# The latent attention layer's opening, started in the layer before and made by halves of the tokens

## The reference, cut to what matters

```
ql = x @ Wqd
q = (ql @ Wqu).reshape(b, t, H, HD).transpose(0, 2, 1, 3)
qr = (ql @ Wqr).reshape(b, t, H, RD).transpose(0, 2, 1, 3)
qr = _apply_rope(qr, cos, sin)          # x*cos + rotate_half(x)*sin
ckv = x @ Wkvd
k = (ckv @ Wku)...; v = (ckv @ Wvu)...
kr = _apply_rope((x @ Wkr)[:, None], cos, sin)[:, 0]
scores = (q·k + qr·kr) * scale, causal; softmax; @ v; @ Wo
```

## Time and profile before

| | us |
|---|---|
| median of three runs | 1404.51 |
| lowest, highest | 1404.14, 1405.84 |
| the profiled execution's own time | 1405.04 |
| its span, first to last instruction | 1403.3 |
| TensorE busy in the span | 1334.0 (95%) |
| latent layer's block starts (trace time) | 976.83 |
| first score chunk of the lead on TensorE | 996.89 |
| first key scores, where the steady loop begins | 1014.26 |

### The profile page before, as it was taken

One profiled execution on the slowest core, in us unless ns is written; L12 is line 12 of the kernel. 1 busy time (PEld: TensorE's weight loads), 2 busy tenths in 40 slices (PEclk: granted clock), 3 DMA queues, 4 the chain that ended last, 5 costly groups with the idle time before them and its releaser, 6 DMA issues. The chain is left out here.

```text
span 1403.3 us, 33400 instructions
## 1 busy us (share of the span) xinstructions
PE 1334.0 (95%) x13987; PEld 754.0 (54%) x13995; DVE 897.1 (64%) x2171; ACT 685.8 (49%) x1035; POOL 278.0 (20%) x343
## 2 busy tenths in 40 slices
PE   8999999999679989999999999999899999999999
PEld 4455556475346775644555564446355555674436
DVE  4899994756486457759999845333656556535331
ACT  5587787646483225546777842111544444442110
POOL 5331513001330000053000000111533433200210
PEclk9999999999879999999999999999999999999999
DMA  4323300000300000032222030001200000000000
GB/s 94 69 37 67 71 8 3 34 1 2 121 1 5 17 1 16 1 63 37 37 36 37 9 113 0 1 0 31 42 14 17 15 14 16 7 2 0 0 0 30
DMA packets 33527, 37.51 MB, mean 27 GB/s; under 512 B 8722, under 2 KB 24194, under 8 KB 33378
## 3 DMA queue, kind: packets, MB, share of 16 engines
q1 hardware_dynamic: 33376, 35.38, 12.3%
q10 hardware_dynamic: 2, 0.00, 0.0%
HBM read 18.43 MB, written 1.07 MB: 14 GB/s over the span
## 5 line engine op out<-in xcount | busy, mean ns | idle before, releaser
L722 DVE TENSOR_REDUCE row_max_pieces<-psum 128x1 f32<-128x512 f32 (+3 forms) x672 | 407.0, 646 | 104.6 <-PE psum L604 102.7
L825 ACT ACTIVATE probs<-psum 128x1024 f32<-128x1024 f32 (+7 forms) x384 | 343.2, 900 | 200.1 <-PE psum L604 199.6
L663 PE MATMUL psum<-probs,v_ones 128*32 128x256 f32 (+1 forms) x2880 | 236.4, 362 | 8.7 <-POOL probs L593 4.3
L604 PE MATMUL psum<-q_all,k_head 97*32 97x512 f32 (+3 forms) x1536 | 177.1, 487 | 0.0
L604 PE MATMUL psum<-k_stack,q_stack 96*32 96x512 bf16 x2048 | 160.2, 380 | 3.4 <-issue 3.3
L604 PE MATMUL psum<-q_stack,k_stack 97*32 97x512 bf16 x2048 | 158.0, 379 | 2.0 <-issue 1.8
L663 PEld LDWEIGHTS psum<-probs,v_ones 128*32 128x32 f32 x2880 | 95.6, 109 | 87.7 <-POOL probs L593 24.2
L604 PEld LDWEIGHTS psum<-k_stack,q_stack 96*32 96x32 bf16 x2048 | 57.6, 96 | 66.6 <-DVE row_max_pieces L722 13.2
L604 PE MATMUL psum<-k_head_bf,q_all_bf 80*32 80x512 bf16 (+3 forms) x768 | 84.1, 329 | 3.2 <-ACT k_head_bf L2800 1.0
L604 PEld LDWEIGHTS psum<-q_stack,k_stack 97*32 97x32 bf16 x2048 | 58.5, 96 | 51.7 <-ACT probs L825 4.3
L604 PEld LDWEIGHTS psum<-q_all,k_head 97*32 97x32 f32 x1536 | 76.0, 109 | 18.1 <-issue 2.0
(11 more groups left out here) (398 smaller groups left out, 2085.9 us busy)
## 6 DMA issues: line engine op xcount, KB each, us to landing
q_stack<-arena SPq DMA_DIRECT2D x32, 96.0 KB, 2.7
k_stack<-arena SPq DMA_DIRECT2D x32, 96.0 KB, 3.0
arena<-gd_g_sums SPq DMA_DIRECT2D x6, 512.0 KB, 6.0
k_stack<-arena SPq DMA_DIRECT2D x32, 64.0 KB, 2.7
q_stack<-arena SPq DMA_DIRECT2D x32, 64.0 KB, 2.7
x_tokens<-in_x SPq DMA_DIRECT2D x4, 256.0 KB, 3.7
k_stack<-arena SPq DMA_DIRECT2D x32, 32.0 KB, 2.0
q_stack<-arena SPq DMA_DIRECT2D x32, 32.0 KB, 2.7
```

The source lines that it names most:

```text
L604: last = pe.matmul(o[j:j + 32], by[:, j:j + 32], rows, **flags)
L663: last = pe.matmul(psum[32 * g:32 * g + VW, PVB, first * P:end * P].rearrange("p (b n) -> p b n", n=P), V[:, c, h, :], by_group(pr[:, n % ...
L722: last = dve.reduce_max(mx[:, h % 2, qt, i:i + 1], o[:, 0:plain], AX.X)
L825: act.activation(pr[:, n % PB, q_from(c):], psum[:, 2 * (n % 2):2 * (n % 2) + 2, :].rearrange("p a n -> p (a n)")[:, q_from(c):], ACT.Exp, ...
```

## The change

Four things, all in code that is written out by hand:

1. `LatentEarly` takes the place of `latent_early`. The rotary query weights and the cosine and sine table are loaded with the latent weights at the start of the routed layer instead of at the start of the latent layer. VectorE turns the rotary weights (`rotate_weights`) in the routed layer, between the last product of the experts' loop and the low-rank down part. The tile `lora_down_second` is dropped, `mask_differences` is used in its place.
2. The latents of the first half of the tokens are made at the end of the routed layer, where `keep_busy` stood.
3. `Prep` is ordered by halves: keys' rotary part, head 0's rotary queries, plain features, casts and the copies of head 0's plain rows for the first 512 tokens, then for the other 512. The first four chunks need the first half only; `wait_rest_of_first` stands before m = 4.
4. Head 1's rotary queries are made after m = 1 in the lead, heads 2 and 3 after m = 5 and m = 9 (were 3 and 7). The values are made after m = 2, and the second plain features after m = 6 (was 5). Of the filler matmuls whose result nobody reads, the two of L2756 go, and of the six of `BUSY` three stay, 256 columns wide instead of 512. The engines' calls `pe_first`, `dve_first` and `act_first` are folded into `pe`, `dve` and `act`.

The diff, cut to its core:

```diff
+                    if m == NT // 2 and rope:
+                        head_loads.wait_rest_of_first(pe)
...
                 if prep:
-                    prep.pe(pe)
-                if rope:
-                    for h in rope.FIRST:
-                        rope_in(h)
-                        prep.pe_first(pe, h)
+                    prep.pe(pe, rope_in)
...
-            d1 = sb2("lora_down_second", [P, S])
+            d1 = MD
...
-            norm = Norm(core, tag, tmp2) if out_dram is None else None
+            norm = Norm(core, tag, tmp2, early=next_layer.early) if out_dram is None else None
...
                             dve.wait_ge(kept, 2 * TOPK * NH2)
+                    if next_layer:
+                        next_layer.rotate_weights(dve)
 
...
+class LatentEarly:
...
+    def loads(self, sp):
+        d = self.d
+        sp.dma_start(self.w1[:, :, 0:3 * LAT], d["w1"].rearrange("(k p) n -> p k n", p=P)).then_inc(self.loaded, 16)
+        for rows in (slice(0, LAT), slice(LAT, P)):
+            sp.dma_start(self.wq[rows, :, 0:RD], d["wqr"].rearrange("p (h n) -> p h n", n=RD)).then_inc(self.loaded, 16)
+        sp.dma_start(self.wplain[0:LAT], d["wqu"]).then_inc(self.loaded, 16)
+        sp.dma_start(self.wplain[LAT:], d["wku"]).then_inc(self.loaded, 16)
+        sp.dma_start(self.cs[:], d["cs"]).then_inc(self.loaded, 16)
+
+    def rotate_weights(self, dve):
+
+        dve.wait_ge(self.loaded, 96)
+        hf, w1, wq = RD // 2, self.w1, self.wq
+        kr, krr = w1[:, :, 2 * LAT:2 * LAT + RD], w1[:, :, 2 * LAT + RD:]
+        dve.tensor_scalar(krr[:, :, 0:hf], kr[:, :, hf:], -1.0, None, ALU.mult)
+        dve.tensor_copy(krr[:, :, hf:], kr[:, :, 0:hf])
+        dve.tensor_scalar(wq[:, :, RD:RD + hf], wq[:, :, hf:RD], -1.0, None, ALU.mult)
+        dve.tensor_copy(wq[:, :, RD + hf:], wq[:, :, 0:hf])
+
+    def latents(self, pe, half):
+
+        for k in range(KT):
+            last = pe.matmul(self.core.psum[:, half, :], self.w1[:, k, 0:2 * LAT],
+                             self.core.XNT[:, k, half * HALF:(half + 1) * HALF], start=(k == 0), stop=(k == KT - 1))
+        last.then_inc(self.l_in, 1)
+
+    def early(self, pe, half):
+        pe.wait_ge(self.loaded, 96)
+        self.latents(pe, half)
...
-                        last.then_inc(kr_in, 1)
+                def key_rotary(pe, half):
+                    if half:
+                        pe.wait_ge(kr_cs, half)
+                    for k in range(KT):
+                        last = pe.matmul(psum[:, KR_BANK, :], w1[:, k, 2 * LAT:], XNT[:, k, cols(half)],
+                                         start=(k == 0), stop=(k == KT - 1))
+                    last.then_inc(kr_in, 1)
+
+                @staticmethod
+                def pe(pe, rope_in):
+                    Prep.key_rotary(pe, 0)
+                    pe.wait_ge(l_out, 1)
+                    rope_in(0, (0,))
+                    for u in (1, 0):
+                        Prep.plain(pe, u, 0)
+                    early.latents(pe, 1)
+                    Prep.key_rotary(pe, 1)
                     pe.wait_ge(l_out, 2)
...
-                    for _ in range(2):
-                        pe.matmul(psum[:, 7, :], ident[:], XNT[:, 0, 0:HALF], start=True, stop=True)
+                    pe.wait_ge(l2_out, 1)
+                    rope_in(0, (1,))
+                    for u in (1, 0):
+                        Prep.plain(pe, u, 1)
+                    pe.wait_ge(kr_cs, 2)
...
                 @staticmethod
                 def pe_between(pe, m):
                     if m in BUSY:
-                        pe.matmul(psum[:, 7, :], ident[:], XNT[:, 0, 0:HALF], start=True, stop=True)
-                    if m == 5:
+                        pe.matmul(psum[:, 7, 0:D], ident[:], XNT[:, 0, 0:D], start=True, stop=True)
+                    if m == 2:
+                        Prep.values(pe)
+                    if m == 6:
                         pe.wait_ge(v_kept, 4)
...
-                def act(act):
+                def act(act, move_rope):
                     for half in range(NH2):
                         act.wait_ge(l_in, half + 1)
                         act.activation(L[:, cols(half)], psum[:, half, :], ACT.Copy).then_inc(l_out, 1)
-                    for half in range(NH2):
                         act.wait_ge(kr_cs, half + 1)
                         act.activation(moved[:, half, :], t[RD:, half, :], ACT.Copy).then_inc(kr_moved, 1)
...
+                        if half == 0:
+                            move_rope(0, (0,))
+                        for u in (1, 0):
+                            Prep.keep_half(act, u, half)
+                        act.wait_ge(kr_added, half + 1)
+                        act.activation(Kb[0:RD, 0, cols(half)], K[0:RD, 0, cols(half)], ACT.Copy).then_inc(kr_copied, 1)
+                    move_rope(0, (1,))
+                    act.activation(Kb[0:RD, 1, :], K[0:RD, 0, :], ACT.Copy).then_inc(kr_copied, 1)
+                    move_rope(1)
...
+                    def cast(half):
+                        for u in (1, 0):
+                            dve.wait_ge(f_kept, NH2 * half + 2 - u)
+                            out, out_b, f = PLAIN[u]
+                            dve.tensor_copy(out_b[:, f, cols(half)], out[:, f, cols(half)]).then_inc(f_cast, 1)
+
+                    by_cs(0)
+                    roped(0, (0,))
+                    add_moved(0)
+                    cast(0)
+                    dve.wait_ge(l_out, 2)
+                    dve.tensor_copy(L2[LAT:, cols(1)], psum[0:LAT, 1, :]).then_inc(l2_out, 1)
+                    by_cs(1)
+                    add_moved(1)
+                    roped(0, (1,))
+                    cast(1)
                     dve.wait_ge(masks_made, 2)
 
                 @staticmethod
...
                                        pattern=[[-1, P]], channel_multiplier=1).then_inc(masks_made, 1)
+                    pool.wait_ge(masks_made, 2)
+                    pool.memset(K[NOPE:SHIFT, :, :], 0.0).then_inc(pads, 1)
+                    pool.wait_ge(pads, 1)
+                    Rope.add(pool, 0, 0)
+                    pool.wait_ge(cast, 1)
+                    pool.memset(K[SHIFT:SHIFT + 1, :, :], 1.0).then_inc(pads, 1)
+                    pool.wait_ge(pads, 2)
+                    Rope.add(pool, 0, 1)
+                    pool.wait_ge(cast, 2)
                     pool.memset(V[:, :, :, HD + 1:], 0.0).then_inc(pads, 1)
-                    pool.memset(V[:, :, :, HD:HD + 1], 1.0).then_inc(pads, 1)
-                    for h in (*Rope.FIRST, *Rope.BETWEEN.values()):
+                    pool.wait_ge(pads, 3)
+                    for h in Rope.BETWEEN.values():
                         for half in range(NH2):
                             Rope.add(pool, h, half)
+                        if h == 1:
+                            pool.wait_ge(cast, NH2 * (h + 1))
+                            pool.memset(V[:, :, :, HD:HD + 1], 1.0).then_inc(pads, 1)
+                            pool.wait_ge(pads, 4)
                     for u in (2, 3):
                         out, out_b, f = PLAIN[u]
                         pool.wait_ge(f_kept, 2 * (u + 1))
                         pool.tensor_copy(out_b[:, f, :], out[:, f, :]).then_inc(f_cast, 1)
...
-            BUSY = range(0, 11, 2)
+            BUSY = (4, 8, 10)
...
-                FIRST, BETWEEN, AT, AHEAD = (0, 1), {3: 2, 7: 3}, 5, 4
...
+                FIRST, BETWEEN, AT, AHEAD = (0,), {1: 1, 5: 2, 9: 3}, 5, 4
...
+                def rows_of_first(sp, half):
+                    for n, (o, f) in enumerate(((Kb, kTb), (Qb, qTb))):
+                        sp.wait_ge(f_cast, NH2 * half + n + 1)
+                        sp.dma_start(o[NOPE:QROWS, 0, cols(half)], f[0:HD, 0, cols(half)]).then_inc(first_rows[half], 16)
...
+                    for half in range(NH2):
+                        HeadLoads.rows_of_first(sp, half)
+                    HeadLoads.keys_bf16(sp, 1)
+                    HeadLoads.queries(sp, 1)
                     sp.wait_ge(q_zeroed, 16)
+                    sp.dma_start(Q[NOPE:QROWS, 0, :], qT[0:HD, 0, :]).then_inc(first_q, 16)
                     sp.wait_ge(pads, 2)
-                    sp.wait_ge(f_cast, 1)
-                    for h in range(2):
-                        HeadLoads.keys_bf16(sp, h)
-                    sp.wait_ge(f_cast, 2)
-                    for h in range(2):
-                        HeadLoads.queries(sp, h)
                     for h in range(2):
                         HeadLoads.keys(sp, h)
                     for h in range(2, 4):
...
-                        pe.wait_ge(kr_copied, 2)
-                    pe.wait_ge(kb_in[h % 2], 16 * (h // 2 + 1))
-                    pe.wait_ge(q_plain[h % 4], 32 * (h // 4 + 1))
+                        pe.wait_ge(kr_copied, 1)
+                        pe.wait_ge(first_rows[0], 32)
+                        pe.wait_ge(cast, 1)
+                        return
+                    if h == 1:
```

(12 more changed lines are left out.)

174 lines of the change are left out of this document (57 added, 117 removed).

## The result

| | before | after |
|---|---|---|
| median on the same chip, us | 1404.10 (eight runs) | 1408.57 (eight runs) |
| lowest, highest | 1401.81, 1405.84 | 1403.47, 1413.23 |
| the profiled execution's own time, its span | 1405.04, 1403.3 | 1405.14, 1403.4 |
| mean granted clock of that execution | 0.984 | 0.979 |
| block's start to first row maximum | 20.35 | 11.2 |

The ratio of after to before is 1.0035, interval 1.0022 to 1.0048: slower by 0.35%, where 0.55% faster was forecast. The opening is shorter by what was forecast, and the lead behind it gives all of that back and more.

A forecast was written before the change was run, and what follows sets the result against it. TensorE, busy 1334.0 of 1403.3 us, was taken as the bound. Opening gain 9.35 less lead loss 1.5 is 7.85, 7.7 kept: 1405.04 becomes 1397.3, less 0.5 for the median 1396.8 us; range 1394.5 to 1401.5.

The forecast's parts named there:

- the lead: From first row maximum to key scores: 18.6 us against 17.1 before, a loss of 1.5 us.
- granted clock: TensorE's clock in the changed stage, expected to stay at 1.00 as in every window before.
- first row maximum: VectorE's first row maximum, expected 11.0 us after the block's start, against 20.35 before.
- The opening: Block's start to first row maximum, worked by halves: 9.35 us gained, or 7.85 if both late casts cost 1.1.
- late casts: VectorE's two casts of the second half's plain features, 0.36 us each while GpSimd waits, up to 1.1 beside it.
- hole ahead of head 1's rotary queries: TensorE's wait in the lead for row maximum 0, before head 1's rotary work: 1.8 us.
- VectorE idle in the values: VectorE running dry in the lead while the values hold TensorE: an idle stretch of 2.5 to 3 us.
- key scores: First key scores on TensorE at the lead's end, expected at 29.6 us after the block's start, against 37.4.
- short waits of VectorE: Waits in the lead behind the values, at the rotary rows and around the second plain features: some 1.5 us.
- the lead gives more back: Rival: handshakes, late casts or a late shift row lose 2 to 4 us more in the lead; 1399.8 us, chance 0.17.
- two rivals: One clock fall of about 4 us in the stage, costing 2 to 4, chance 0.07; low clock over the lead, 0.05.
- The third rival: Clock stays low over the lead, chunks 0 to 13, only three narrow fillers left: 12 lost, 1408.8 us, chance 0.05.

The follow-up runs named there:

- e1: Changed kernel with two 512-wide fillers after the lead's first chunk, ahead of head 1's rotary queries; median 1396.35 us, ratio to before 0.9970.
- e11: Kernel before without the two fillers ahead of the values, the lead's six kept; median 1406.40 us, ratio to before 1.0033.
- e3: Kernel before without the two fillers ahead of the values, the lead's six cut to three 256 wide; median 1405.47 us, ratio to before 1.0026.
- e10: Kernel before with its eight fillers of opening and lead on 64 rows instead of 128; median 1407.25 us, ratio to before 1.0051.
- e2: Changed kernel with the lead's six 512-wide fillers of before put back; median 1399.60 us, ratio to before 0.9970.
- e5: Changed kernel with two 512-wide fillers after the first chunk and the lead's three made 512 wide; median 1395.72 us, ratio to before 0.9948.
- e9: Changed kernel with two fillers after the first chunk and three in the lead, all 512 wide on 64 rows; median 1396.66 us, ratio to before 0.9970.
- e4: Kernel before with only the early loads, weight turning and first latents in the routed layer, opening undivided; median 1400.75 us, ratio to before 0.9979.
- e7: Changed kernel with two 512-wide fillers after the first chunk and no others in the lead; median 1405.21 us, ratio to before 1.0012.
- e8: Changed kernel with the lead's three fillers 512 wide, nothing added after the first chunk; median 1404.92 us, ratio to before 1.0016.

## Why the prediction was wrong

By its own steps, in us from the block's start; e1 stands beside, since it is the changed kernel at full clock, with two fillers added:

| step | forecast | after | e1 |
|---|---|---|---|
| turning the weights | up to 6.8, hidden | 2.1, hidden | |
| latents early, in the filler's place | 1.84 for 1.88 | 1.88 | |
| first chunk on TensorE | 9.4 | 9.6 | 9.6 |
| late casts, each | 0.36 | 0.42 | |
| first row maximum | 11.0 | 11.2 | 11.2 |
| hole ahead of head 1's rotary queries | 1.8 | 1.57 | filled |
| values | 3.72 | 7.19 | 3.72 |
| VectorE idle in the values | 2.5 to 3 | 6.32 | 2.45 |
| key scores | 29.6 | 38.6 | 31.0 |
| granted clock | 1.00 | 0.50 for 20 us | 1.00 |
| head 0 to head 1 | 13.7 | 13.67 | |

**The opening was right**, in size (9.15 us gained, 9.35 forecast) and in its steps. Both figures lean on the one trace of before, in which the table came 1.94 us late; with e11's landing the gain would be about 7.2, with e3's about 10.3. The casts beside GpSimd took 1.19 and 0.82, the first just above the upper bound of 1.1, and were hidden as forecast; the late one, alone, took 0.42, near its 0.36. The Trainium skill's rule of the locked port pair (SBUF — State Buffer, "SBUF: two separate sides") agrees with the first of them, which ran beside GpSimd's sum of 981.86 to 983.12.

**The lead was mis-sized by 1.2 us at full clock.** Forecast were 18.6 us from first maximum to key scores; e1 took 31.0 - 11.2 = 19.8. The values end at 17.0 where 16.3 was forecast; 0.4 of that are e1's own fillers, which put head 1's rotary queries at 11.9 instead of 11.5. Behind the values the sum had 1.5 us of short waits of VectorE; the three that the trace shows are 0.81, 0.97 and 0.81, 2.6 together, two of them for the rotary queries of heads 2 and 3. That is the rival "the lead gives more back", at 1.2 of the 3 us that it was priced at.

**The step that failed is the clock.** The sum had it at 1.00 throughout, and its loss stood only in two rivals with 0.12 of the chance between them. The third rival named the place (the lead), the price (12 lost, 1408.8) and the cause (only three narrow fillers left), and gave it 0.05; the median is 1408.57. That its price fits to 0.2 us is in part luck: the trace shows 7.5 us for the clock, and the lead's own 1.2 are in the difference. Two arguments against it were wrong:

- "the values and rotary matmuls, 128 or 64 rows by 256 to 512 columns, take their place." They didn't. The values ran for 7.19 us without a gap at 0.50 and the clock did not come back, and e10 shows fillers on 64 rows to hold it less well. The values have 64 rows in the trace, the rotary matmuls run in pairs of 64. That they hold the clock less well than fillers of 128 is argued from e10; no run swaps them alone.
- "the hole of 1.96 us at L2727 and those of 0.78 and 1.02 drew no fall." True, but between the first of them and the last stood two full-width fillers of 128 rows (990.03 to 992.01), and behind the last the first filler of the lead. Taking the two alone out of the kernel before (e11) makes it slower by 0.33%. The rows of before showed a stage held up by what the change takes away, so they were no evidence for a stage without it.

The Trainium skill says that the clock follows how busy TensorE has recently been (TensorE: Matmul & The Clock Gate, "The HAM clock gate"); I cited that as speaking against the change and gave it no term in the sum. e1, e2 and e5 agree with its direction. But if busy is read as time in flight, the traces do not: 19.19 of 20 us in flight at 0.50, and e10 falls with TensorE as busy as before.

**The numbers.** In the two profiled executions the clock's 7.5 us and the lead's 2.8 (19.84 in e1 against 17.08 before) turn a gain of 9.15 into a loss of 1.1 at the key scores. The median loses 4.5. The traced run is the second fastest of eight; the two slowest (1413.2) have a mean clock of 0.972 against its 0.979. That difference over 1,400 us is as much as 20 us more at 0.50 (0.007 x 1400 / 0.5), so I infer longer or further falls in those runs; none was traced. Where the clock is kept, the stage is worth somewhat less than the forecast 7.8: the key scores come 6.4 us earlier in e1 and 5.8 in e5. The medians gain 6.4 in e1, three slow runs in it, 7.65 in e5 (from 1403.37) and 5.6 in e9 (from 1402.30). That e5's figure meets the forecast of 7.7 is luck: its trace shows only 5.8 of it in this stage, and where its runs gained the rest isn't shown.

**What stays open.** What the chip weighs when it lowers and restores the clock: neither idle time nor rows alone order all these kernels, and each kernel has one trace, so falls in other runs are read from their mean clock. Whether the hole that the late table leaves in the kernel before, in e3, e10 and e11 helps a fall is untested. Why e4 falls shortly with eight fillers in it is not shown either.

## What to carry to other kernels

Before a stage is made shorter or fillers are taken out, look at what keeps TensorE's clock up in it: matmuls that look like waste may carry the stage, and a row of before with them in place says nothing about the clock without them. Fill the waits that TensorE has anyway with matmuls of 128 rows: that costs next to nothing (0.6 us in e5 for three wider ones, nothing for the two ahead of the values in before) and was worth 9 us (e5 against e7 and e8). Before a difference of one or two microseconds between two traces is put down to an edit, look for a load that landed earlier in one of them. Then look at the granted clock by windows in the changed kernel, and at the mean clock of several runs, since one traced run can keep a clock that most others lose.

## What the runs showed of the hardware

- The clock stayed at 0.50 for 20 us with TensorE in flight for 19.19 of them (after, 990 to 1010), and for 13 us with it in flight throughout (e7, 1009 to 1022, for the most part float32 key scores of 97 rows in tiles of 32 columns). The same work at the same place runs at 1.00 in before (1014.26 to 1028.00). Being in flight does not bring the clock back soon, but neither does this work lower it.
- Fillers of the same length on 64 rows instead of 128 made the kernel before slower by 0.5%, with a mean clock of 0.56 over 10 us of its trace (e10).
- A fall behind a hole of 1.57 us cost 7.5 us (after against e1). In the times of one and the same kernel, runs of lower mean clock took about 12 us more (e1: seven runs around 1395, three at 1405.5 to 1409.1).
- The load of the cosine and sine table, 512 KB at the block's start, took 7.2 us from issue to landing in before, 8.4 in e3 and 5.3 in e11; VectorE waited 1.94 us, 3.13 and not at all for it.
- Three short float32 matmul groups on different row halves (rotary queries and both plain features, six records of 512 columns) took 1.91 us together in after, from 979.19 to the next group's start at 981.10; the prediction had taken 2.05.
